# Two decoder layers on one core: early weights, identity products across barriers, a gather merged by halves, and an input scale found before the FFN

## The chip, the cores and the metric

The kernel runs on one core of a Trainium2 chip. The metric is the device time of one execution in microseconds (us); lower is better. The five engines of the core are TensorE (PE), VectorE (DVE), ScalarE (ACT), GpSimd (POOL) and SyncE (SP), which here only issues transfers.

## The reference

Sixteen sequences of 256 tokens with 256 features pass through two decoder layers. Each has self-attention (16 heads of 16 features), cross-attention to a context of 77 tokens, and a feed-forward part (FFN), each ahead of a residual sum and behind a layernorm without weights:

```python
x = x + attn(norm(x), window 64, w_qkv, w_out)     # L0 self-attention, |i - j| <= 32
x = x + xattn(norm(x), ctx, padding mask per batch) # L0 cross-attention
x = x + moe(norm(x))                                # L0 FFN: 8 experts, top 2, 256-512-512-256, gelu
x = x + attn(norm(x), causal)                       # L1 self-attention
x = x + xattn(norm(x), ctx, mask of 256 x 77)       # L1 cross-attention
x = x + ffn(norm(x))                                # L1 FFN: weights of 4 bits, activations of 16 bits
# every quantisation of the L1 FFN has one scale for the whole tensor:
scale = max(max(abs(t)) / 32767, 1e-12); q = clip(round(t / scale), -32768, 32767) * scale
```

## The kernel before

The program has five parts, each an `nc.Block` in which every engine has its own stream of instructions; at the end of a block all engines meet at a barrier. Semaphores order the engines inside a block.

1. `layers` fills constants: GpSimd clears `v_aug` and `eye` and sets the ones columns, VectorE derives `selects` and `to_all` from the identity matrix, SP loads the first item of `x`.
2. `attention(..., "window", "cross_pad", route=...)` runs layers 1 and 2 as one software pipeline and also normalises the result, finds each token's two experts and scatters its rows into regions of DRAM (`route`).
3. `experts` runs 71 tiles of 128 rows. A tile's expert weights (2.18 MB) are loaded whole into a ring of four; the first expert's parts are loaded at the end of part 2. It also quantises the raw weights of the last FFN and starts the gather of the first item's results (`gather_first`, four indirect transfers, two for each half of 128 tokens).
4. `attention(..., "causal", "cross_mask", merge=..., tail=...)` runs layers 3 and 4 in the same pipeline. It merges the experts' rows (`merge_rows`), and in its `tail` normalises the result, turns it into `x_sb` (`last_turn` on TensorE, `keep_turned` on ScalarE) and keeps a peak of absolute values for each item (`tail.peak`).
5. `quantised_ffn` finds the scale of its input from these peaks (`across`, `scale`), quantises `x`, and then runs gate, up and down products with a whole-tensor peak between each.

The attention pipeline has steps `ref` = 0, 1, ...; there are N = 32 items (16 sequences for each of two layers). In step `ref` item `ref` is projected (Q, K, V), item `ref`-1 gets its first scores and row maxima, item `ref`-2 its second scores, exponentials and P*V, item `ref`-3 its output transposes and output projection, item `ref`-4 its residual sum (`add_output`) and, in the tail, its last layernorm, and item `ref`-5 is turned. Each step has eight sub-steps `i`, and every engine runs `step(t, ref)` in this order, which is written out by hand. Sub-steps of full steps are in a hardware loop (`Fori`), the first and last ones are written out. Q and K are stacked through SP: 16 transfers a step from `parts` to `q_pair` and `k_pair`. Identity products (`keep_warm`) fill waits of TensorE at the start of part 4 (START_WARM, 16 calls), at the end of part 2 (END_WARM, 24) and in the FFN (BEFORE_GATE, 6, and others). A call is one fp32 product of 128x128 and shows as two instructions.

## Time and profile before

| | |
|---|---|
| median of 3 runs | 2162.05 us (2161.76 to 2166.89) |
| profiled execution | 2154.5 us |
| its span, first to last instruction | 2152.9 us |
| TensorE busy | 1999.5 us, 93% |
| VectorE, ScalarE, GpSimd busy | 1247.8, 964.2, 691.5 us |
| mean granted TensorE clock | 0.979 of full |
| part 1 | 0 to 5.8 us |
| part 2 | 5.8 to 659.5 us |
| part 3 | 659.5 to 1193.5 us |
| part 4 | 1193.5 to 1822.2 us |
| part 5 | 1822.2 to 2152.9 us |

The profile is of one execution. Its instructions carry start and duration, the idle time of the engine before them, and what ended that wait. A timeline merges like instructions that follow each other; "x8" is their count, and the duration then spans them all. An fp32 product shows as two instructions. TensorE's clock has two levels, 1.2 and 2.4 GHz. Queue rows (SPq) are the issue of a transfer, not its run.

### The profile page before, as it was taken

What the parts mean: (1) busy time and instruction counts of PE and PEld (TensorE: products, weight loads), DVE (VectorE), ACT (ScalarE), POOL (GpSimd) and SP (SyncE); (2) the same over time, 40 slices, a digit from 0 to 9 for tenths busy, and PEclk for the clock granted to TensorE, in tenths of its full rate; (3) what the DMA queues carried; (4) which work ended last, traced back from release to release, by engine and by line L of the source; (5) the groups of instructions that cost most, each with busy time, mean ns of one, the idle gap of its engine ahead of it and who ended that gap; (6) DMA issues with size and microseconds to landing.
All of it is one profiled execution on the core that took longest, in us unless ns stands there. A gap on an engine that the chain in (4) does not pass through costs nothing. (4 is left out here: it accounts for less than half of the span.)

```text
span 2152.9 us, 51243 instructions
## 1 busy us (share of the span) xinstructions
PE 1999.5 (93%) x17250; PEld 1544.5 (72%) x17250; DVE 1247.8 (58%) x5456; ACT 964.2 (45%) x1873; POOL 691.5 (32%) x1246
## 2 busy tenths in 40 slices
PE   7999998999968999999999889999999997999889
PEld 5777776666647999999999567777766664444377
DVE  5788886666641011111015588888778785459964
ACT  3455545666622333333333255555555553357410
POOL 3666665345561000000000555553322220013410
PEclk9999999999968999999999999999999998999999
DMA  7333333333319999999996633343223331000023
GB/s 219 107 110 103 112 110 94 93 108 116 115 60 359 370 344 341 337 350 337 341 346 242 193 123 126 124 134 112 90 89 108 105 101 36 0 0 1 0 60 97
DMA packets 209540, 334.50 MB, mean 155 GB/s; under 512 B 59501, under 2 KB 193426, under 8 KB 200306
## 3 DMA queue, kind: packets, MB, share of 16 engines
q1 hardware_dynamic: 194914, 301.82, 40.4%
q0 software_dynamic: 9552, 26.10, 4.0%
q10 hardware_dynamic: 4928, 4.72, 0.6%
q8 instruction: 82, 1.34, 0.3%
q14 instruction: 64, 0.52, 0.1%
HBM read 193.74 MB, written 28.05 MB: 103 GB/s over the span
## 5 line engine op out<-in xcount | busy, mean ns | idle before, releaser
L1978 ACT ACTIVATE moe_h<-moe_h_ps,moe_weights 128x128 f32<-128x128 f32 x424 | 132.8, 364 | 258.6 <-PE moe_h_ps L1948 226.1
L1293 ACT ACTIVATE causal_prob<-causal_ps 128x768 f32<-128x768 f32 (+1 forms) x192 | 169.0, 880 | 110.6 <-PE causal_ps L1546 109.7
L2416 PE MATMUL ffn_prod_ps<-x_sb,ffn_weights 128*128 128x512 f32 x480 | 209.2, 595 | 7.0 <-ACT ffn_sig_q L2402 7.0
L2010 DVE TENSOR_TENSOR moe_y<-moe_y_ps,moe_weights 128x256 f32<-128x256 f32 x53 | 22.5, 425 | 328.2 <-PE moe_y_ps L1960 328.2
L1891 POOL DMA_DIRECT2D moe_y_dram<-moe_y x71 | 39.4, 555 | 496.2 <-DVE moe_y L2010 496.2
L1948 PE MATMUL moe_h_ps<-moe_h,moe_weights 128*128 128x128 f32 x1696 | 198.0, 275 | 0.0
L1948 PEld LDWEIGHTS moe_h_ps<-moe_h,moe_weights 128*128 128x128 f32 x1696 | 193.6, 192 | 0.1
L2416 PEld LDWEIGHTS ffn_prod_ps<-x_sb,ffn_weights 128*128 128x128 f32 x480 | 90.5, 190 | 123.5 <-issue 109.2
L1010 DVE CUSTOM_DVE_ANT_0 causal_masked<-causal_ps,causal_causal_mask 128x256 bf16<-128x256 f32 (+1 forms) x512 | 152.4, 353 | 40.2 <-PE causal_ps L1512 38.2
L1010 DVE CUSTOM_DVE_ANT_0 window_masked<-window_ps,window_window_mask 128x160 bf16<-128x160 f32 x512 | 135.2, 319 | 58.2 <-PE window_ps L1512 55.7
L1293 ACT ACTIVATE window_prob<-window_ps 128x640 f32<-128x640 f32 x128 | 90.0, 703 | 97.1 <-PE window_ps L1546 96.2
L805 POOL TENSOR_SCALAR_AFFINE_SELECT causal_prob<-causal_prob 128x512 f32<-128x512 f32 x128 | 85.3, 691 | 115.0 <-ACT causal_prob L1293 114.9
L1512 PEld LDWEIGHTS causal_ps<-k_pair,q_pair 64*128 64x128 f32 x1024 | 72.0, 185 | 66.9 <-issue 33.1
L1512 PE MATMUL causal_ps<-k_pair,q_pair 64*128 64x78 f32 (+2 forms) x1024 | 98.1, 293 | 18.1 <-DVE causal_m_tok L1010 15.9
L2267 DVE TENSOR_REDUCE ffn_peak<-ffn_wide 128x1 f32<-128x1024 f32 x72 | 87.0, 1210 | 47.9 <-ACT ffn_wide L2376 47.9
L1512 PE MATMUL window_ps<-k_pair,q_pair 64*128 64x160 f32 (+1 forms) x1024 | 99.3, 295 | 16.2 <-DVE window_m_tok L1010 16.1
L1010 DVE CUSTOM_DVE_ANT_0 causal_masked<-causal_ps,causal_cross_mask 128x77 bf16<-128x77 f32 x512 | 86.2, 235 | 47.0 <-PE causal_ps L1512 46.9
L1512 PEld LDWEIGHTS window_ps<-k_pair,q_pair 64*128 64x128 f32 x1024 | 74.0, 187 | 49.9 <-DVE window_m_tok L1010 28.1
L1930 PE MATMUL moe_h_ps<-moe_rowsT,moe_weights 128*128 128x128 f32 x848 | 105.0, 278 | 2.5 <-DMA moe_weights<-moe_w_in 2.5
L792 POOL TENSOR_SCALAR_AFFINE_SELECT window_prob<-window_prob 128x384 f32<-128x384 f32 (+1 forms) x128 | 74.8, 608 | 94.6 <-ACT window_prob L1293 94.5
L1930 PEld LDWEIGHTS moe_h_ps<-moe_rowsT,moe_weights 128*128 128x128 f32 x848 | 100.4, 194 | 2.7 <-DMA moe_weights<-moe_w_in 2.7
L1960 PE MATMUL moe_y_ps<-moe_weights,moe_h 128*128 128x256 f32 x424 | 100.4, 380 | 0.7 <-ACT moe_h L1978 0.7
(389 smaller groups left out, 4694.2 us busy)
## 6 DMA issues: line engine op xcount, KB each, us to landing
moe_weights<-moe_w_in SPq DMA_DIRECT2D x53, 2180.0 KB, 9.3
q_pair<-parts SPq DMA_DIRECT2D x512, 128.0 KB
parts<-moe_w_in SPq DMA_DIRECT2D x17, 2180.0 KB, 9.0
k_pair<-parts SPq DMA_DIRECT2D x256, 128.0 KB
k_pair<-parts SPq DMA_DIRECT2D x256, 38.5 KB
moe_y_dram<-moe_y POOLq DMA_DIRECT2D x71, 128.0 KB, 3.5
moe_rows<-moe_slots_dram SPq DMA_DIRECT2D x53, 128.0 KB, 3.5
x_before_ffn_dram<-x_sb SPq DMA_DIRECT2D x16, 256.0 KB, 2.2
```

What stands on the lines that cost most here:

```text
L792: op = nc.gpsimd.affine_select(out=m, in_=m, compare_op=ALU.is_ge, fill=0.0, base=base, pattern=[[0, 4], [1, width]], channel_multiplier=-1)
L805: op = nc.gpsimd.affine_select(out=m, in_=m, compare_op=ALU.is_ge, fill=0.0, base=0, pattern=[[0, 4], [1, P]], channel_multiplier=-1)
L1010: op = nc.vector.tensor_tensor_reduce(masked[:, junk * width:junk * width + nk_real], ps1[:, ab, p * L.width1 + col:p * L.width1 + col + n ...
L1293: nc.scalar.activation(out, src, ACT.Exp).then_inc(expd, 1)
L1512: op = nc.tensor.matmul(ps1[:, ab, j * L.width1 + col:j * L.width1 + col + nk], q_pair[par][rows_of[ab], i + j, qt * P:qt * P + P], k_pair ...
L1891: pool.dma_start(route.y_dram[bass.ds(j * TM, TM), :].rearrange("(s p) d -> p s d", p=P), y[r][:])\
L1930: op = nc.tensor.matmul(h1_ps[:, f // 2, (f % 2) * TM:(f % 2) * TM + TM], w1[:, k, f * P:f * P + P], rowsT[:, k, :], start=(k == 0), stop= ...
L1948: op = nc.tensor.matmul(h2_ps[:, f // 2, (f % 2) * TM:(f % 2) * TM + TM], w2[:, k, f * P:f * P + P], h1[:, k, :], start=(k == 0), stop=(k ...
L1960: op = nc.tensor.matmul(y_ps[:, r % YR, s * D:s * D + D], h2[:, k, s * P:s * P + P], w3[:, k, :], start=(k == 0), stop=(k == FB - 1))
L1978: nc.scalar.activation(out[:, f, :], psum[:, f // 2, (f % 2) * TM:(f % 2) * TM + TM], ACT.Gelu, bias=bias[:, f:f + 1]).then_inc(done, 1)
L2267: return nc.vector.tensor_reduce(out, rows, AX.XY, ALU.max, apply_absolute_value=True)
L2416: op = nc.tensor.matmul(prod_ps[:, slot, f, :].rearrange("p (b t) -> p b t", b=2), w[:, k, at:at + P], x_cols(n // GROUPS, k), start=(k == ...
```

## The change

- The Q and K weights of layers 1 and 3 get tensors of their own (`first_wq`, `first_wk`). SP loads those of layer 1 in part 1, behind the first item of `x`, and those of layer 3 in part 3, at tile 7, behind the raw FFN weights. SP's other loads of part 4 stand behind the wait for the first gather's second half.
- TensorE gets identity products in part 1 (6 calls), at the head of part 2 (LOAD_WARM, 6), at the head of part 3 (FIRST_WARM, 7), and in the emptying steps of part 4 (DRAIN_WARM, 4 and 2). END_WARM goes from 24 to 13. BEFORE_GATE goes from 6 to 4 and stands at the head of part 5.
- One of the two `v_aug` tensors is filled by VectorE. In both attention parts GpSimd begins `constants()` only after the first normalisation.
- The first item's gather signals by halves of 128 tokens (`half_in`, `got_in`), and VectorE merges the first half before it waits for the second.
- In the tail's emptying steps (`emptied`, `ref` >= N + 2) the two turns of rows go to two PSUM banks (`turn_bank`), without waits between them. In step N + 3 the peak comes behind the statistics.
- The FFN's input scale is found in the last step of part 4 (`input_scale`), and kept in `tail.scales` and `tail.inverse`.
- In steps in which `ref`-1 is an item of layer 4, `add_output` comes before the first row maximum instead of after it.

```diff
 class Tail:
-    def __init__(self, rows_dram, peak):
+    def __init__(self, nc, ctx, rows_dram, peak):
         self.rows_dram, self.peak = rows_dram, peak
+        self.scales, self.inverse = (ctx.enter_context(nc.sbuf_tensor(f"ffn_{n}", [P, 5], F32)) for n in ("scales", "inverse"))
...
-        START_WARM, END_WARM = 16, 24
+        START_WARM, END_WARM, LOAD_WARM, DRAIN_WARM = 16, 13, 6, 4
...
+        def emptied(ref):
+
+            return bool(tail) and ref >= N + 2
+
+        def turn_bank(ref, k):
+
+            return ps1[:, k, 0:S] if emptied(ref) else bank(0)[:, S:2 * S]
...
+                if merge:
+                    sp.wait_ge(got_in[0], 32)
                 load_layer(0)
                 if load:
                     x_view, _, x_second, x_loaded = load
                     sp.dma_start(x_sb[:, ST:TILES // 4, :], x_view[:, ST:TILES // 4, :]).then_inc(x_second, 16)
-                if merge:
-                    sp.wait_ge(got_in[0], 64)
-                    sp.wait_ge(wq_in, 16)
...
                 layernorm(0, 0)
-                if merge:
-                    pool.wait_ge(normed, 1)
+                pool.wait_ge(normed, 1)
                 constants()
...
+                def input_scale():
+
+                    one, top_one = tail.scales[:, 0:1], row_top[:, 1:2]
+                    dve.wait_ge(peak_found, 2)
+                    nc.vector.reduce_max(whole_top[:], tail.peak[:], AX.X).then_inc(peak_found, 1)
+                    dve.wait_ge(top_turned, 1)
+                    nc.vector.reduce_max(top_one, ps2[0:1, 0, 0:P], AX.X).then_inc(top_spread, 1)
+                    dve.wait_ge(top_row, 1)
+                    nc.vector.tensor_scalar(one, ps2[:, 1, 0:1], 1.0 / QMAX, LEAST, ALU.mult, ALU.max).then_inc(top_scaled, 1)
+                    dve.wait_ge(top_scaled, 1)
+                    nc.vector.reciprocal(tail.inverse[:, 0:1], one)
...
+                    if isinstance(t, int) and t == 0:
+                        s, k = n // 2, n % 2
+                        if n % 2 == 0:
+                            dve.wait_ge((merge.half_in, got_in[0])[s], 32)
+                        else:
+                            dve.wait_ge(merged, n)
...
+                        added_first = active(ref, 4) and active(ref, 1) and layer_at(ref, 1).kind == "cross_mask"
+                        if i == 0 and added_first:
+                            add_output(t, ref, 4)
                         if active(ref, 1):
                             row_max(t, ref, i)
-                        if i == 0 and active(ref, 4):
+                        if i == 0 and active(ref, 4) and not added_first:
                             add_output(t, ref, 4)
...
-                        if i == 1 and tail and in_tail(ref, 5):
+                        if i == (3 if ref == N + 3 else 1) and tail and in_tail(ref, 5):
...
                     if ref == 0 and merge:
-                        pe.wait_ge(got_in[0], 64)
+                        pe.wait_ge(got_in[0], 32)
                         keep_warm(START_WARM)
+                    if ref == 0 and load:
+                        keep_warm(LOAD_WARM)
...
+                        if i == 3 and ref == STEPS - 1 and tail:
+                            pe.wait_ge(peak_found, 3)
+                            nc.tensor.transpose(ps2[0:1, 0, 0:P], whole_top[:], ident[:]).then_inc(top_turned, 1)
                         if i == 4 and in_tail(ref, 5):
-                            pe.wait_ge(last_ev, tail_item(t, 5) * 2 + 1)
+                            if not emptied(ref):
+                                pe.wait_ge(last_ev, tail_item(t, 5) * 2 + 1)
...
                         if i == 5 and active(ref, 3):
                             pe.wait_ge(o_ev, t - 2)
-                            if in_tail(ref, 5):
+                            if in_tail(ref, 5) and not emptied(ref):
                                 pe.wait_ge(last_ev, tail_item(t, 5) * 2 + 2)
...
                         if i == 6 and active(ref, 3):
+                            if emptied(ref):
+                                keep_warm(DRAIN_WARM, ps2)
                             pe.wait_ge(o_norm, t - 2)
...
                         if i == 7 and active(ref, 3):
+                            if emptied(ref):
+                                keep_warm(DRAIN_WARM // 2, ps2)
                             pe.wait_ge(oT_ev, t - 2)
...
+                if tail:
+                    pe.wait_ge(top_spread, 1)
+                    nc.tensor.matmul(ps2[:, 1, 0:1], ones_row[:], row_top[:, 1:2], start=True, stop=True).then_inc(top_row, 1)
...
+                        if j == RING + 3:
+                            for n, name in enumerate(("Wq", "Wk")):
+                                sp.dma_start(early[n][:], a[f"L1_attn_{name}"].rearrange("(k p) n -> p k n", p=P))\
+                                  .then_inc(early[2], 16)
...
-                                .then_inc(route.got_in, 16)
+                                .then_inc((route.half_in, route.got_in)[s], 16)
...
+                    for _ in range(FIRST_WARM):
+                        nc.tensor.matmul(h2_ps[:, 0, 0:P], ident[:], ident[:], start=True, stop=True)
                     tiles(pe, tile)
...
-BEFORE_GATE, BEFORE_PEAK, BEFORE_DOWN = 6, 20, 6
+BEFORE_GATE, BEFORE_PEAK, BEFORE_DOWN = 4, 20, 6
...
-                nc.vector.reduce_max(top[:, X_:X_ + 1], x_peak[:], AX.X).then_inc(found[0], 1)
-                across(0, 1)
-                scale(X_, 1.0)
...
+                keep_warm(BEFORE_GATE)
                 pe.wait_ge(ones_ready, 1)
-                across(0, X_, 1)
-                keep_warm(BEFORE_GATE)
...
+                for n in range(2):
+                    sp.dma_start(early[0][n][:], a["L0_attn_w_qkv"][:, n * D:n * D + D].rearrange("(k p) n -> p k n", p=P))\
+                      .then_inc(early[0][2], 16)
+
+            @block.tensor
+            def _(pe):
+                for _ in range(6):
+                    nc.tensor.matmul(first_ps[:, 0:P], ident[:], ident[:], start=True, stop=True)
...
-                for i in range(2):
-                    nc.gpsimd.memset(v_aug[i][:], 0.0)
                 nc.gpsimd.memset(eye[:], 0.0).then_inc(filled, 1)
-                pool.wait_ge(filled, 1)
-                for i in range(2):
-                    op = nc.gpsimd.memset(v_aug[i][:, :, :, HD:HD + 1], 1.0)
-                op.then_inc(filled, 1)
+                nc.gpsimd.memset(v_aug[0][:], 0.0).then_inc(filled, 1)
+                pool.wait_ge(filled, 2)
+                nc.gpsimd.memset(v_aug[0][:, :, :, HD:HD + 1], 1.0).then_inc(filled, 1)
...
+                nc.vector.memset(v_aug[1][:], 0.0).then_inc(v_zeroed, 1)
                 dve.wait_ge(filled, 1)
```

## Rows read from the trace of the kernel before

**Rows 1.** The page, part 1: the engines.

```profile
...
PE 1999.5 (93%) x17250; PEld 1544.5 (72%) x17250; DVE 1247.8 (58%) x5456; ACT 964.2 (45%) x1873; POOL 691.5 (32%) x1246
...
```

**Rows 2.** Timeline, 0 to 45 us: start, length, engine, line [idle before, releaser].

```profile
...
1.95 1.84 POOL L2533 MEMSET v_aug<- 128x1024 f32 x2 [0.31 <-POOLq L2493]
...
5.35 0.22 DVE L2553 CAST to_all<-picked 128x128 bf16<-128x128 f32 x1
...
8.17 2.70 DVE L87 TENSOR_SCALAR window_xn<-x_sb,window_mv,window_rstd 128x256 f32<-128x256 f32 x2 [1.11 <-POOL window_rstd L55]
...
12.88 3.75 PE L1668 MATMUL window_misc<-window_xT,window_window_wq 128*128 128x256 f32 x8 [0.84 <-ACT window_xT L1382]
...
19.47 2.57 SPq L609 DMA_DIRECT2D q_pair<-parts  x4
...
29.43 0.45 PE L1512 MATMUL window_ps<-k_pair,q_pair 64*128 64x160 f32 x4
...
```

**Rows 3.** Line 87 alone from 0 to 60 us: count, then ns min/median/max.

```profile
...
L87 DVE TENSOR_SCALAR window_xn<-x_sb,window_mv,window_rstd x6: 395/408/2381, 8.2 to 47.7; 128x256 f32<-128x256 f32 x6
...
```

**Rows 4.** Timeline across the barrier into the experts, 634 to 690 us.

```profile
...
650.93 8.37 PE L1445 MATMUL window_ps<-ident 128*128 128x128 f32 x48 [7.00 <-ACT moe_logits L1437]
...
661.46 0.33 SPq L1876 DMA_DIRECT2D moe_weights<-moe_w_in  x1
...
670.10 3.57 PE L1930 MATMUL moe_h_ps<-moe_rowsT,moe_weights 128*128 128x128 f32 x16 [2.47 <-DMA moe_weights<-moe_w_in]
...
679.14 1.95 PE L1930 MATMUL moe_h_ps<-moe_rowsT,moe_weights 128*128 128x128 f32 x16
...
```

**Rows 5.** Transfers of expert weights, 655 to 680 us: issue to landing.

```profile
...
DMA to landing us min/median/max: 8.6/12.8/15.9
```

**Rows 6.** One window, 680 to 1180 us: length, busy us (count), clock, DMA share.

```profile
...
680.00:1180.00 500.00, 500.00 (x3966) 482.43 (x3966) 75.42 (x161) 171.65 (x548) 37.76 (x68) 1.00 0.92 340
...
```

**Rows 7.** Timeline across the barrier into the second attention part, 1160 to 1235 us.

```profile
...
1193.58 0.95 POOL L1903 DMA_INDIRECT moe_got<-moe_y_dram,moe_got_pos  x1 [0.30 <-POOLq L1864]
...
1197.73 6.27 PE L1445 MATMUL causal_ps<-ident 128*128 128x128 f32 x32 [5.07 <-DMA moe_got<-moe_y_dram,moe_got_pos]
...
1199.85 0.95 POOL L746 DMA_INDIRECT causal_got<-moe_y_dram,causal_got_pos  x1 [0.30 <-issue]
...
```

**Rows 8.** Gathers and loads into got: issue to landing.

```profile
...
DMA to landing us min/median/max: 2.2/3.3/5.5
```

**Rows 9.** Timeline of one step of the last layer, 1746 to 1764 us, VectorE.

```profile
...
1748.96 0.24 DVE L1010 CUSTOM_DVE_ANT_0 causal_masked<-causal_ps,causal_cross_mask 128x77 bf16<-128x77 f32 x1 [1.32 <-PE causal_ps L1512]
...
1750.23 0.68 DVE L1028 TENSOR_TENSOR x_sb<-x_sb,causal_misc 128x512 f32 x1
...
```

**Rows 10.** Timeline of the same step, TensorE.

```profile
...
1751.01 1.97 PE L1668 MATMUL causal_misc<-causal_xT,causal_cross_mask_wq 128*128 128x256 f32 x8 [0.29 <-issue]
...
```

**Rows 11.** TensorE waits, 1540 to 1780 us: total us, times, longest.

```profile
...
PE causal_ps L1512 <- DVE causal_m_tok L1010: 4.4, 14, 0.5
PE causal_misc L1668 <- issue: 4.0, 13, 0.5
...
```

**Rows 12.** Timeline, 1802 to 1845 us: emptying steps, start of the FFN.

```profile
...
1804.91 1.02 ACT L1391 ACTIVATE causal_o_aug<-causal_pso 128x1024 f32<-128x1024 f32 x1 [1.77 <-PE causal_pso L1568]
...
1807.33 1.12 PE L1739 MATMUL causal_misc<-ident,causal_o_aug 64*128 64x64 f32 x16 [0.63 <-ACT x_sb L1351]
...
1811.15 3.78 PE L1763 MATMUL causal_misc<-causal_cross_mask_wo,causal_oT 128*128 128x256 f32 x8 [0.69 <-ACT causal_oT L1356]
...
1819.41 0.69 DVE L1185 TENSOR_REDUCE x_peak<-causal_last_xn 128x1 f32<-128x512 f32 x1
...
1822.35 0.17 DVE L2269 TENSOR_REDUCE ffn_top<-x_peak 128x1 f32<-128x16 f32 x1 [2.25 <-PEq L526]
...
1824.84 0.75 DVE L2274 TENSOR_SCALAR x_sb<-x_sb,ffn_inverse 128x1024 f32<-128x1024 f32 x1
...
1826.88 18.50 PE L2416 MATMUL ffn_prod_ps<-x_sb,ffn_weights 128*128 128x512 f32 x42
...
```

91 lines of the change are left out of this document (58 added, 33 removed).

## The prediction

> **What bounds the kernel now.** I read the page first. TensorE is busy for 1999.5 of 2152.9 us and no other engine reaches 60% [rows 1]. So a gain must come from TensorE's idle time, from stretches in which it runs at the lower of its two clock levels (1.2 instead of 2.4 GHz), or from the places where one part of the program ends and the next begins. I then read the timelines of these places: the start [rows 2, 3], the way into the experts and the experts [rows 4 to 6], the way into the second attention part [rows 7, 8], one step of the last layer [rows 9 to 11], and the emptying steps with the start of the FFN [rows 12]. TensorE is the engine that the others wait for in all long stages between them, so an advance at a joint should last to the end, and the terms add up.
>
> **Part A, the start.** The first block ends when VectorE has written to_all (5.35 + 0.22 = 5.57 us), after GpSimd has filled both v_aug tensors (1.84 us for two) [rows 2]. After the change GpSimd fills one and VectorE the other. Half of 1.84 us, 0.9, leaves GpSimd, and about as much is added to VectorE ahead of its own chain of 1.6 us; TensorE gets six identity products that must end before the block does. Nothing shows a VectorE memset of that size. If the two fills pass each other freely the block is 0.8 us shorter, if they exclude each other 0. I take 0.3. The reason is the normalisation: two instructions took 2.70 us [rows 2], although such an instruction has a median of 408 ns and one took 2381 [rows 3]; that was the one beside GpSimd's memsets in constants(). The change holds constants() back until this normalisation is done, so 2.38 - 0.41 = 2.0 us go. constants() itself ends about 0.4 us later than now, and what needs it (the bias product) comes far behind.
>
> For the two fills in the first block the Trainium skill has another answer: "SBUF — State Buffer", section "Who interferes with whom", says that on this chip a VectorE instruction with at most one SBUF input outside its two-port modes does not contend with GpSimd. By that rule the fills would be free of each other and part A would gain 0.5 us more than I take.
>
> TensorE thus gets its first rows 2.3 us earlier. The first eight Q products took 3.75 us at the low level; the same eight of shape 128x256 take 1.97 in [rows 10]. The identity products ahead of them (12 instructions in each of two blocks) may lift the clock: up to 1.8 us for Q and another 0.9 for K. Against this, VectorE's statistics of the second item wait for x, ahead of the low part of Q in the same queue, and SP issues the first q_pair transfer only at 19.47, right after its last load [rows 2]. Both come earlier by what leaves SP's queue in this block (two weights of about 0.5 us each) and by the shorter start: 1.8 to 2.3 us. TensorE's first scores (29.43) are then 1.8 us earlier if these loads and a low clock bind, 4.2 if nothing binds. I take **3.0**.
>
> **Part B, into the experts.** The 24 identity products take 8.37 us [rows 4] and end last before the barrier, at 659.3. Thirteen of them, all at the low level, would take about 5.8 us (26 instructions of some 0.22: the 8.37 us hold some 27 low and 21 high ones), so the barrier falls 2.5 us earlier. Seven new ones stand behind it, while the first rows are still in flight. SP's first transfer of whole expert weights starts 2.5 us earlier than 661.46, and TensorE's wait for it (2.47 us, until 670.10) ends 2.5 us earlier. In place of 2.47 us of idle there is then about 0.9, and the clock need not fall: the sixteen products took 3.57 us there and 1.95 later [rows 4], so another 1.6. Together 4.1; I take **4.0**. Lower bound 2.5 (the clock falls anyway). Upper bound 4.8: the third transfer took up to 15.9 us [rows 5], and the next layer of products at 679.14 has only some 2.7 us to spare. The two early loads of Wq and Wk (0.5 MB) go behind the raw FFN weights into the same queue. TensorE is busy for all of the 500 us from 680 on [rows 6], so I cost them at nothing; if that cover were gone they would cost some 1.3 us once.
>
> **Part C, into the second attention part.** Today TensorE waits for the four gathers until 1197.73, does 16 identity products (6.27 us) and turns the first rows right behind them [rows 7]. With the weights of layer 3 already there and SP silent until the gathers land, the last gather (issued 1193.58) has the DMA engines to itself. It took 4.1 us; such transfers take 2.2 us at the least and 3.3 in the median [rows 8], and I expect it between these. The identity products then end 0.8 to 1.9 us earlier. VectorE merges the first half meanwhile, which takes 0.9 us out of its chain, but GpSimd is busy issuing the next item's gathers until 1199.85 + 0.95 = 1200.80 and only then computes the deviation, as it does now about 0.3 us later. So the rows are normed only 0.3 us earlier, at 1202.6, and TensorE can turn them 1.2 us earlier at most. I take **0.9**, with 0 and 1.2 as bounds. The layer's other loads start later, behind the gathers; their first user comes 8 us on.
>
> **Part D, the last layer's steps.** This edit is not in the change's name: add_output moves ahead of the first row maximum where layer 4 runs, 16 steps. VectorE is idle for 1.32 us before that maximum, the addition takes 0.68 us [rows 9], and what it waits for (the output projection) is complete before the scores are. It fits into the hole. TensorE's Q products wait for the addition: 0.29 us in this step [rows 10], 4.0 us over 13 steps [rows 11]. The value is 0.29 per step, 16 x 0.29 = 4.6. Early steps show other waits, so **4.3**. The waits for the row maxima (4.4 us in 14 [rows 11]) I leave: VectorE is idle again before the maximum that starts that chain, so the chain moves with TensorE. If they went too, the part would bring 8.4; if another wait took the place, 0.
>
> **Part E, emptying steps and FFN start.** o_aug is ready at 1804.91 + 1.02 = 1805.93, but its transposes start at 1807.33, behind ScalarE's two copies of turned rows, which now have PSUM banks of their own: 1.3 us. The output projection takes 3.78 us [rows 12] where eight such products take 1.97 [rows 10]: 1.8 us, and 0.6 for the two sets of transposes before it, if the new identity products (4 and 2) hold the clock. They lie in the waits for VectorE and ScalarE. Moving the peak behind the statistics takes 0.6 us out of the chain. At the joint the peak ends at 1820.1, VectorE idles 2.25 us until 1822.35 and quantises x from 1824.84 [rows 12]. In the new order the reduction starts at once and the barrier (some 0.4 us) follows it; the chain is shorter by two small instructions and longer by a turn of rows ahead of its last product: 2.0 us saved. The first gate products wait for two identity products fewer: 0.4. Sum 6.7. What is late next is the clock: until now 12 identity instructions and the long chain lifted it about when the gate products began. Now these begin after eight. They take 18.50 / 42 = 0.44 us each [rows 12], twice that at the low level; if they run low for 1.2 to 4.6 us longer, half of it is lost, so I subtract 1.4. That gives 5.3 with the clock held, 2.8 without. I take **4.4**, nearer to the first.
>
> **The sum** is 3.0 + 4.0 + 0.9 + 4.3 + 4.4 = 16.6 us. The profiled execution took 2154.5 us (its span 2152.9 and 1.6 around it), so that one becomes 2137.9. The median of the runs shown is 7.5 us above it, 2162.05; against it I predict 2145.4.
>
> **The rivals.** *The clock stays low at the joints* (chance 0.2): A 1.8, B 2.5, C 0.5, D 4.3, E 2.8, sum 11.9, 2150.2. For it speaks that the identity products are few and that the clock fell beside 2.47 us of idle; against, that the idle stretches shrink everywhere. *Every wait goes* (0.13): A 4.2, B 4.8, C 1.2, D 8.4, E 5.3, sum 23.9, 2138.2. For it, VectorE is 0.6 us ahead in each step; against, its idle time before the second maximum eats this. *The reordering in layer 4 does nothing* (0.08): 12.3 us, 2149.8; TensorE's Q products would then wait for the turned rows instead, which are ready some 0.6 us earlier. *Slower* (0.04): the raw weights and the early loads together (2.9 MB) hold back the experts' weights. It decides once a transfer lands more than 2.7 us later than now; each tile concerned then costs 2.5 us of wait and 1.6 of low clock. Five tiles would cancel the gain, eight end at 2162 + 33 - 17 = 2178. Against it: TensorE had no idle time in 500 us [rows 6], with the raw weights in them.
>
> **Chances.** The forecast has 0.55; its own range is 2140 to 2151. The range for 8 in 10 takes in the second and third case and the bounds of the clock: 2135 to 2155. About 0.3%, 6.5 us, is what a measurement of this kernel can tell from no change. Below 2155.6 lie nearly all of the first four cases: faster 0.88, same 0.08, slower 0.04.
>
> **What the new profile would show.** A: first normalisation about 0.8 us long, first scores near 26.4. B: 26 identity instructions before the barrier, the second tile's first layer in about 1.95 us. C: the identity products behind the gathers start about 1 us earlier. D: no wait before Q in layer 4, steps of 15.55 instead of 15.85 us. E: output projection of the last item in 2 us, gate products some 5 us earlier relative to the last step. Wrong would make me: Q, K or the last projection still near 3.7 us, a new wait for weights after 670 us, or steps of layer 4 as long as before.

## The result, and the profile after

| | before | after |
|---|---|---|
| median of four runs | 2163.24 us (2161.76 to 2166.89) | 2147.17 us (2145.92 to 2150.1) |
| profiled execution, its span | 2154.5, 2152.9 us | 2145.92, 2144.3 us |
| ratio of the times | | 0.9928, 95% interval 0.9916 to 0.9940 |

By the medians the change takes 16.1 us off, and the interval of the ratio is 13 to 18 us; 16.6 were forecast, and the median lies 1.8 us above the predicted 2145.4. But the two profiled executions differ by 8.6 us only, and the sum of the prediction was made on a profile. So the first question is, stage by stage, where the time went, and the second why the pair of profiles shows half of it.

The page of the changed kernel, part 1, beside [rows 1]. TensorE is busy for nearly as long as before (2001.3 us against 1999.5), so the gain lies in its idle time.

```profile
...
PE 2001.3 (93%) x17274; PEld 1546.4 (72%) x17274; DVE 1247.5 (58%) x5456; ACT 963.5 (45%) x1873; POOL 689.7 (32%) x1244
...
```

**Part A.** Timeline of the changed kernel, 0 to 31 us, beside [rows 2, 3].

```profile
...
2.09 0.95 POOL L2605 MEMSET v_aug<- 128x1024 f32 x1
2.24 0.91 DVE L2611 MEMSET v_aug<- 128x1024 f32 x1 [2.24 <-PEq L2553]
...
7.47 0.74 DVE L87 TENSOR_SCALAR window_xn<-x_sb,window_mv,window_rstd 128x256 f32<-128x256 f32 x2 [1.11 <-POOL window_rstd L55]
...
8.45 2.39 DVE L948 TENSOR_SCALAR window_window_bq<-window_window_bq 128x2 f32<-128x2 f32 x1
...
10.90 3.78 PE L1716 MATMUL window_misc<-window_xT,first_wq 128*128 128x256 f32 x8 [1.98 <-DVE window_window_bq L948]
...
17.60 2.57 SPq L627 DMA_DIRECT2D q_pair<-parts  x4
18.46 0.88 DVE L993 SCALAR_TENSOR_TENSOR parts<-window_misc,window_window_bk,parts 128x256 fp32r<-128x256 f32 x2 [1.93 <-ACT parts L1307]
...
27.59 0.45 PE L1558 MATMUL window_ps<-k_pair,q_pair 64*128 64x160 f32 x4
...
```

In the row names, Q and K are each written to `parts` in two parts: ScalarE writes the high part, and VectorE (L993) the low part, which is what the high part leaves over. "K's low part" below is that instruction, 18.46 to 19.34 us here; it has nothing to do with the clock.

The two fills of `v_aug` ran side by side, 0.95 us on GpSimd and 0.91 on VectorE, where two on GpSimd took 1.84. By the rule of the Trainium skill ("SBUF — State Buffer", section "Who interferes with whom") they are free of each other; the trace agrees. The normalisation shrank from 2.70 to 0.74 us, as forecast. But `constants()` now begins right behind it, and VectorE's next instruction but one, the scaling of the two columns of `bq`, takes 2.39 us. It ends at 10.84 us, when the fifth of GpSimd's memsets there, which run from 8.27 us on, has ended at 10.82. Q waits 1.98 us for it. The blocking had moved on to another instruction. The first scores come 1.84 us earlier.

**Part B.** Timeline across the barrier into the experts, beside [rows 4].

```profile
...
658.01 4.99 PE L1491 MATMUL window_ps<-ident 128*128 128x128 f32 x26 [7.00 <-issue]
...
664.28 1.28 ACT L2044 ACT_TABLE_LOAD   x1 [6.18 <-PEq L544]
664.33 1.80 PE L2029 MATMUL moe_h_ps<-ident 128*128 128x128 f32 x14 [1.33 <-PEq L544]
...
674.64 2.05 PE L1994 MATMUL moe_h_ps<-moe_rowsT,moe_weights 128*128 128x128 f32 x16 [1.04 <-DMA moe_weights<-moe_w_in]
...
682.04 1.95 PE L1994 MATMUL moe_h_ps<-moe_rowsT,moe_weights 128*128 128x128 f32 x16
...
```

In the kernel before, ScalarE's first instruction behind the barrier was this one:

```profile
...
659.68 1.28 ACT L1978 ACT_TABLE_LOAD   x1 [8.65 <-PEq L526]
...
```

Thirteen products stand ahead of the barrier in place of 24, seven behind it. From the first of them to ScalarE's table load it takes 664.28 - 658.01 = 6.3 us, where it took 659.68 - 650.93 = 8.8. TensorE waits 1.04 us for weights in place of 2.47, and the second tile's first layer takes 2.05 us in place of 3.57, near the 1.95 of the third tile.

**Part C.** Timeline across the barrier into the second attention part, beside [rows 7].

```profile
...
1196.48 0.94 POOL L1967 DMA_INDIRECT moe_got<-moe_y_dram,moe_got_pos  x1 [0.30 <-POOLq L1924]
...
1199.26 6.36 PE L1491 MATMUL causal_ps<-ident 128*128 128x128 f32 x32 [3.71 <-DMA moe_got<-moe_y_dram,moe_got_pos]
...
1205.45 0.63 PE L1663 MATMUL causal_misc<-ident,causal_xn 128*128 128x128 f32 x4
...
1213.39 0.59 ACT L1349 ACTIVATE causal_cross_mask_ctxT<-causal_ps 128x512 f32<-128x512 f32 x1
...
1215.09 0.60 ACT L1349 ACTIVATE causal_cross_mask_ctxT<-causal_ps 128x512 f32<-128x512 f32 x1 [1.11 <-PE causal_ps L1504]
...
1217.13 4.80 PE L1520 MATMUL causal_ps<-causal_cross_mask_ctxT,causal_cross_mask_wk 128*128 128x462 f32 x8 [0.81 <-ACT causal_cross_mask_ctxT L1349]
...
```

From the issue of the last gather to TensorE's start it takes 1199.26 - 1196.48 = 2.8 us; it was 1197.73 - 1193.58 = 4.15. The rows are turned 16.92 us behind the last output product of the experts, where it was 18.20. But then ScalarE copies the first piece of the turned context and stands idle for 1.11 us with the second piece turned already, and the context products of layer 4, 3.11 us in the kernel before, take 4.80: the clock has fallen.

**Part D.** TensorE's waits in layer 4 of the changed kernel, 1543.48 to 1777.53 us (total us, times, longest), beside [rows 11]. These are its two largest.

```profile
...
PE causal_ps L1558 <- DVE causal_m_tok L1029: 3.9, 14, 0.5
PE causal_misc L1669 <- ACT causal_oT L1402: 1.9, 10, 0.2
...
```

The wait ahead of Q, 4.0 us in 13 times before, is not in the list any more. Each of the last ten steps takes 15.46 us; in the kernel before they take 15.82 on average.

**Part E.** Timeline of the emptying steps and the start of the FFN, beside [rows 12].

```profile
...
1803.64 0.72 PE L1791 MATMUL causal_misc<-ident,causal_o_aug 64*128 64x64 f32 x16 [0.65 <-ACT causal_o_aug L1437]
...
1806.84 1.99 PE L1819 MATMUL causal_misc<-causal_cross_mask_wo,causal_oT 128*128 128x256 f32 x8
...
1815.98 0.75 DVE L2335 TENSOR_SCALAR x_sb<-x_sb,ffn_inverse 128x1024 f32<-128x1024 f32 x1 [0.38 <-PEq L544]
...
1817.82 11.47 PE L2477 MATMUL ffn_prod_ps<-x_sb,ffn_weights 128*128 128x512 f32 x25
...
```

The transposes follow `o_aug` at once, the last output projection takes 1.99 us in place of 3.78, and the quantising of x begins 8.86 us earlier, 2.24 of which item 31's scores had brought along.

**Stage by stage.** The start of TensorE's first instruction of each stage (VectorE's for the quantising) cuts the span. Lengths in us, from the windows view of each profile. "Again" is a second profile of the same kernel (the first two experiments), "timed" a third one of the changed kernel (further down).

| up to | before | before, again | after | after, again | after, timed |
|---|---|---|---|---|---|
| first scores of part 2 | 29.43 | 28.64 | 27.59 | 26.25 | 27.54 |
| scores of item 4 | 76.63 | 76.62 | 76.62 | 83.39 | 76.62 |
| scores of item 23 | 347.33 | 347.90 | 347.12 | 347.08 | 347.22 |
| scores of item 31 | 130.23 | 138.30 | 134.22 | 134.91 | 134.53 |
| identity products at its end | 67.31 | 71.33 | 72.46 | 72.51 | 69.67 |
| first output product, part 3 | 22.53 | 22.11 | 18.51 | 18.75 | 18.45 |
| last output product | 512.17 | 512.48 | 512.01 | 512.01 | 512.02 |
| first rows turned, part 4 | 18.20 | 18.50 | 16.92 | 16.94 | 16.88 |
| first scores of part 4 | 13.95 | 13.65 | 16.41 | 16.31 | 16.43 |
| scores of item 4 | 80.46 | 81.85 | 79.74 | 80.70 | 79.72 |
| scores of item 15 | 223.34 | 223.51 | 223.30 | 223.33 | 223.32 |
| scores of item 31 | 258.19 | 258.27 | 252.63 | 252.42 | 252.85 |
| quantising of x | 45.07 | 44.55 | 38.45 | 38.35 | 38.40 |
| first gate product | 2.04 | 2.04 | 1.84 | 1.84 | 1.84 |
| end | 326.01 | 327.27 | 326.47 | 327.57 | 327.40 |

In the first pair of profiles the kernel before is (134.22 + 72.46) - (130.23 + 67.31) = 9.1 us better in layer 2 and the emptying behind it, where nothing was changed. The places that the change touches give 1.84 + 4.02 + 5.56 + 6.82 us, less 0.5 over the three stages of the way into part 4 (down to "scores of item 4").

### The profile page after: what moved, and what is told of

Read it like the earlier page. It is cut to its first block and busy times, and to the rows that moved or that the text cites. A ratio compares the mean times of both kernels' runs of the same rounds, so it can differ in the third digit from the quotient of the medians.

```text
span 2144.3 us, 51295 instructions
## 1 busy us (share of the span) xinstructions
PE 2001.3 (93%) x17274; PEld 1546.4 (72%) x17274; DVE 1247.5 (58%) x5456; ACT 963.5 (45%) x1873; POOL 689.7 (32%) x1244
```

## The experiments

**The kernel before, profiled again (before_again).** No edit.

> The kernel before, profiled a second time. In its first profile layer 2's steps are 16.28 us apart and part 3 computes its first tile's output (first moe_y) at 678.45 us less 2.9; the changed kernel's steps there are 16.65 us apart, and it loses 8.95 us between the first scores of the start and the end of part 2. Theory 1 (these two profiles met different executions of the same work): this profile of the kernel before shows steps of about 16.65 us in layer 2 as well, and a span near 2160 us, in line with its median. Theory 2 (the change itself slows layer 2): steps of 16.28 us again, a span near 2153 us.

It took 2168.73 us, its span 2167.0. The windows view from item 23's scores to item 31's (length, busy us and count of PE, PEld, DVE, ACT, POOL, then clock, DMA share, GB/s), first of the first profile, then of this one:

```profile
...
453.39:583.62 130.23, 123.63 (x1379) 89.37 (x1380) 84.48 (x330) 82.36 (x153) 76.20 (x174) 1.00 0.38 118
...
```

```profile
...
453.16:591.46 138.30, 126.75 (x1379) 91.34 (x1380) 84.49 (x330) 82.55 (x153) 76.22 (x174) 0.98 0.36 112
...
```

The same instructions and a longer stretch: the first profile had steps of 16.28 us throughout, this one 16.7 to 17.0 and two of 18.6 and 18.8 at a lower clock. Theory 1 holds, though the span was expected near 2160: the 9.1 us belong to the execution that the first profile caught and not to the change. The 27 other times measured of the kernel before say the same: none is below 2160.81 us, and the first profile's is 2154.5. Whether the changed kernel ever has such an execution is open: in its own profiles and in those of the experiments below the stretch takes 134.2 to 139.6 us. TensorE's wait for VectorE's `o_tok` is 0.4 us in the short steps and up to 1.1 in these; what sets it was not followed further.

**The changed kernel, profiled again (after_again).** No edit.

> The changed kernel, profiled a second time. Theory 1 (the steps of layer 2 vary from execution to execution): steps there anywhere from 16.28 to 16.65 us. Theory 2 (the change slows them): 16.65 us again. In part 4, ScalarE's wait of 1.11 us before its second copy of the turned context, and the context products of layer 4 at 4.80 us: if they come from where the loads of part 4 now stand, both are there again and the first scores come about 1.2 us later behind the first expert outputs than in the kernel before; if they belong to that one execution, they are gone and the first scores come about 1 us earlier.

It took 2153.98 us. Layer 2 has steps of 16.7 us again, and the way into part 4 is as in the first profile, ScalarE's stop and the low clock with it. New is the second line of the table, 83.39 us. Timelines of SP and of TensorE:

```profile
...
29.58 4.13 SPq L590 DMA_DIRECT2D x_sb<-x_in  x3
33.82 5.22 SPq L627 DMA_DIRECT2D q_pair<-parts  x4
...
```

```profile
...
26.25 0.45 PE L1558 MATMUL window_ps<-k_pair,q_pair 64*128 64x160 f32 x4 [0.84 <-DMA k_pair<-parts]
...
46.51 0.55 PE L1558 MATMUL window_ps<-k_pair,q_pair 64*128 64x160 f32 x4 [1.98 <-DMA k_pair<-parts]
...
```

SP puts the three 1 MB loads of the rest of x into its queue right behind step 0. Issuing them took 4.13 us, and the four q_pair transfers behind them 5.22, where four take 2.6 with nothing in the way. TensorE waits 1.98 us for k_pair, and the clock falls behind the wait: the steps took 20.26, 20.24 and 23.20 us instead of 18.22, 17.70 and 21.01. In this execution Q ran at the high level (1.99 us in place of 3.78), so the scores were 1.3 us earlier and met those loads.

**Part D undone (add_behind_max).**

```diff
-                        added_first = active(ref, 4) and active(ref, 1) and layer_at(ref, 1).kind == "cross_mask"
+                        added_first = False
```

> The changed kernel with part D undone: add_output stands behind the first row maximum again in layer 4. Theory (part D is worth what the wait of TensorE's Q products was, plus what follows from it): steps 18 to 30 at 15.82 us instead of 15.46, in all 4.6 to 5.6 us more from the first scores of step 16 to those of step 31. Rival (the steps became shorter for another reason, e.g. the earlier weights): steps stay at 15.46 us, 0 us.

From item 15's to item 31's scores it takes 257.51 us, 4.9 more than the mean of the changed kernel (252.63). The last ten steps are 15.79 us long, and the wait ahead of Q is back (4.1 us, 13 times). The theory holds. The 0.7 us that are left to the 258.2 of the kernel before are not of this edit.

**constants() later (constants_later).**

```diff
                 pool.wait_ge(normed, 1)
+                if route:
+                    pool.wait_ge(scaled[0], 1)
                 constants()
```

> The changed kernel with GpSimd's constants() in part 2 held back until VectorE has scaled bq too, so that neither the normalisation nor the 2.39 us scaling of bq runs beside GpSimd's memsets. Q products should start near 9.9 us instead of 10.90. Theory (SP's queue of loads, which ends at 17.5 us, sets when the first q_pair transfer is issued, 17.60): the first scores stay at 27.6 us, within 0.2. Rival (the scaling of bq sets the start): the first scores come 1.0 us earlier, or 2.5 to 3 if the clock holds through Q as well.

```profile
...
8.46 0.16 DVE L950 TENSOR_SCALAR window_window_bq<-window_window_bq 128x2 f32<-128x2 f32 x1
...
9.77 1.97 PE L1718 MATMUL window_misc<-window_xT,first_wq 128*128 128x256 f32 x8 [0.84 <-ACT window_xT L1430]
...
18.82 2.58 SPq L627 DMA_DIRECT2D q_pair<-parts  x4
...
```

The scaling of `bq` took 0.16 us, so GpSimd's memsets beside it had cost 2.2. Q starts 1.13 us earlier and at the high level, and still the first scores come at 26.65, later than the 26.25 above. Neither expectation fits: the theory had 27.6, and the rival's 1.0 us is met in number, but with Q at the high level it had 2.5 to 3. SP issued its last load at 18.43 and q_pair at 18.82. Two lines fit the six profiles up to here within 0.2 us. The first scores come 8.27 us behind the end of K's low part (29.43 = 21.16 + 8.27; 27.59 = 19.34 + 8.25) or some 7.95 us (7.8 to 8.1) behind the first q_pair issue (26.25 = 18.19 + 8.06; 26.65 = 18.82 + 7.83), whichever is later. The first binds when Q runs low, SP's queue when it runs high.

**The rest of x, one load a step (x_loads_spread).**

```diff
-                    if load and ref == 0:
-                        for n in range(1, 4):
+                    if load and ref < 3:
+                        for n in range(ref + 1, ref + 2):
```

> The changed kernel with the three 1 MB loads of the rest of x issued one behind each of steps 0, 1 and 2 of part 2 instead of all three behind step 0. In the profiles of the changed kernel the issue of the third load took up to 2.65 us and that of the next q_pair transfer up to 3.20 us, and TensorE waited 2.0 us for k_pair, at a lower clock behind it: from the first scores to those of item 4 it took 76.61, 83.39, 78.43 and 80.17 us, where the kernel before took 76.63 twice. Theory (an earlier start meets SP's queue while it is filled by these loads): no q_pair issue in step 1 above 1.2 us, no wait for k_pair, 76.6 us or a little less. Rival (the lower clock there has another cause): still 78 us or more.

It takes 82.65 us from the first scores to item 4's, as the rival says. The steps say more: the first two took 18.22 and 17.70 us, as short as any, and the third 27.05. There VectorE stood before this row of its timeline:

```profile
...
74.31 0.75 DVE L75 BATCH_NORM_STATS2 window_stats<-x_sb 128x6 f32<-128x256 f32 x2 [5.77 <-DMA x_sb<-x_in]
...
```

The edit issued the last load behind step 2, at 68.80 us, and its first user needed it before it could land. It made a wait of its own of 5.77 us, so the run decides nothing about the theory. The last two runs below put the loads behind step 1.

**Fewer identity products (fewer_identity).** FIRST_WARM 7 and DRAIN_WARM 4 become 0.

> The changed kernel without the seven identity products at the head of part 3 and without those in the emptying steps of part 4. Theory of the prediction: (1) in part 3 the clock falls, so that from the first identity product at the end of part 2 to the first output product it takes 1 to 1.6 us more than 18.5; (2) the output projection of the last item goes back from 1.99 to 3.8 us and the joint from the scores of item 31 to the quantising of x takes 40.3 to 40.9 us instead of 38.4. Rival (the products do nothing, the shorter waits alone hold the clock): 18.5 us and 38.4 us.

```profile
...
667.81 3.65 PE L1994 MATMUL moe_h_ps<-moe_rowsT,parts 128*128 128x128 f32 x16 [0.61 <-DVE moe_rowsT L2063]
...
```

```profile
...
1809.20 3.78 PE L1819 MATMUL causal_misc<-causal_cross_mask_wo,causal_oT 128*128 128x256 f32 x8 [0.69 <-ACT causal_oT L1402]
...
```

The first tile's first layer takes 3.65 us in place of 2.02, and the stage 20.18 in place of 18.57 (mean of three). The last projection is back at 3.78 us, and from item 31's scores to the quantising it takes 40.44 us, 2.0 more. Both prices of a low clock are as forecast. Each kernel with an edit has one profile; in the nine other profiles with the same products at this place the first stage takes 18.2 to 19.5 us (20.2 in freed_queues, see there).

**Identity products where they were (more_before_barrier).** END_WARM 24, LOAD_WARM 0, BEFORE_GATE 0.

> The changed kernel with END_WARM back at 24, no identity products ahead of the first block's rows in part 2 (LOAD_WARM 0), and none ahead of the gate products (BEFORE_GATE 0). Theory of the prediction: (1) from the first identity product to the first output product 2.5 us more (21.0 us); (2) Q at the start at the low level, 3.75 us, the first scores at 27.6 us as in the first profile of the changed kernel, since SP's queue bounds them; (3) the gate products begin up to 0.4 us earlier and run low for some us, which costs 0 to 1.5 us until the end of the first gate products. Rivals: (1) the barrier is set by something else, 18.5 us; (2) the clock at the start is worth 1.4 us, first scores 27.6 against 26.2; (3) the clock is up at the gate anyhow, 0.

```profile
...
661.31 7.35 PE L1491 MATMUL window_ps<-ident 128*128 128x128 f32 x48 [7.01 <-issue]
669.08 1.80 PE L2029 MATMUL moe_h_ps<-ident 128*128 128x128 f32 x14 [0.42 <-PEq L544]
...
```

(1) 24 products took 7.35 us where 13 took 4.99, but the stage grew by 1.6 us only, to 20.16, and not to the expected 21.0: behind 13 products TensorE stands 1.33 us at the barrier until another engine is there, behind 24 only 0.42. The same 24 products had taken 8.37 and 8.46 us in the two profiles of the kernel before, so this run undoes only 1.4 of the 2.45 us by which the barrier had moved; why they were shorter here was not followed. (2) The first scores come at 27.45, with Q low, as expected. That alone doesn't price the products: with them Q was low from end to end in four of the seven executions in which it started at 10.9 us, and high in all four in which it started at 9.8. (3) The gate products start 0.2 us earlier; the granted clock of their first 3 us is 0.76, in the changed kernel 0.81, in the kernel before 0.90. Against the kernel before the change thus pays 3 x (0.90 - 0.81) = 0.3 us of clock there.

**SP's loads ahead of the wait (loads_before_wait).**

```diff
+                load_layer(0)
                 if merge:
                     sp.wait_ge(got_in[0], 32)
-                load_layer(0)
```

> The changed kernel with SP's loads of layer 3 (wv, wo) issued at once in part 4, ahead of the wait for the first gather's second half, as before; all later loads stay behind the wait. From the last expert output to the turn of the first rows it takes 16.9 us, 18.2 to 18.5 in the kernel before. Theory (SP's silence lets the last gather land sooner): 0.5 to 1.2 us more, 17.4 to 18.1. Rival (the order of the merge and the 32 instead of 64 to wait for are what brought it): 16.9 still. ScalarE's stop of 0.4 to 1.1 us between copies of the turned context, and the low clock behind it: if the loads that stand close behind the gather cause it, it is smaller here; if it comes from ScalarE itself, it is there again.

```profile
...
1199.88 0.95 POOL L1967 DMA_INDIRECT moe_got<-moe_y_dram,moe_got_pos  x1 [0.30 <-POOLq L1924]
...
1204.24 5.67 PE L1491 MATMUL causal_ps<-ident 128*128 128x128 f32 x32 [5.26 <-DMA moe_got<-moe_y_dram,moe_got_pos]
...
```

The last gather is issued at 1199.88 and TensorE starts at 1204.24, 4.36 us later; with SP silent it was 2.8. The rows are turned 17.79 us behind the last output product: as the theory has it, SP's silence is worth 0.9 us there, and the rest of part C (18.35 - 17.79) 0.6. ScalarE's stop shrank to 0.1 us, and its second copy again began 18.3 us behind its table load at the head of part 4.

**The changed kernel, timed (after_timed).**

> The changed kernel, timed in five rounds beside the kernel before, as the mark for the run behind it. Summed from the stages of the profiles so far, (start 2.4 minus what steps 1 to 3 give back, way into the experts 3.7, way into part 4 0.3, layer 4 5.3, emptying and joint 6.6), it should be 13 to 18 us faster than the kernel before, near 2148 to 2150 us. If the gain of the first profile of the changed kernel was luck, it is below 10 us.

2146.31 us (2144.51 to 2149.84) against 2162.82, ratio 0.9932, interval 0.9918 to 0.9946. The gain is there again, 16.5 us.

**Other queues (freed_queues).** In part 2 ScalarE issues the context's loads and one weight before its first copy and three weights behind it, `constants()` is later, and loads 2 and 3 of the rest of x stand behind step 1. In part 4 START_WARM is 10, and

```diff
-                    gather(1, 1)
+                    gather(1, 1, range(0, 2))
                 layernorm(0, 0)
+                if merge:
+                    gather(1, 1, range(2, 4))
```

> The changed kernel with five edits. In part 2: constants() behind the scaling of bq; ScalarE issues the loads of the context and of layer 2's four weights instead of SP; the second and third load of the rest of x stand behind step 1. In part 4: GpSimd issues two of item 1's four gathers, then computes item 0's deviation, then issues the other two; START_WARM 10 instead of 16. Theory: the first scores come 8.27 us after the low part of K or 7.95 us after SP's first q_pair issue, whichever is later: with SP's queue shorter by some 5 us they come at 25.3 us when Q runs at the high clock, and steps 1 to 3 take 76.6 us; in part 4 the first rows are turned 15.0 us after the last output product instead of 16.9. Together 2.5 to 5 us faster than the changed kernel. Rival (the loads only change queues and x lands later; the shorter row of identity products leaves the clock low): start as now or later, 26.2 us or more; the turn in part 4 comes earlier but the products behind it take twice as long, 0 us in all.

2156.06 us (2151.95 to 2157.93), ratio to before 0.997 (0.9957 to 0.9982): 10 us slower than the changed kernel. The rival won, at both places.

```profile
...
5.36 0.50 ACTq L1494 DMA_DIRECT2D indow_cross_pad_ctx_rows<-ctx_in  x1
...
8.62 0.41 SPq L575 DMA_DIRECT2D x_sb<-x_in  x1
...
20.07 0.75 DVE L75 BATCH_NORM_STATS2 window_stats<-x_sb 128x6 f32<-128x256 f32 x2 [10.99 <-DMA x_sb<-x_in]
...
31.71 0.45 PE L1579 MATMUL window_ps<-k_pair,q_pair 64*128 64x160 f32 x4
...
```

```profile
...
1217.78 1.08 ACT L1360 ACTIVATE causal_cross_mask_ctxT<-causal_ps 128x512 f32<-128x512 f32 x2
1221.16 0.60 ACT L1360 ACTIVATE causal_cross_mask_ctxT<-causal_pso 128x512 f32<-128x512 f32 x1 [2.29 <-remote]
...
```

ScalarE's loads went out at 5.36 us, ahead of SP's load of x at 8.62. VectorE stood idle for 10.99 us until x was there at 19.98 (13.92 in the changed kernel), and the first scores came at 31.71. The edits in part 2 are several, but this chain shows the one that cost the time. In part 4 the turn came 14.94 us behind the last output product, 2.0 earlier, as forecast. But ScalarE then stops for 2.29 us between its copies of the context, and the first scores come 17.41 us behind the turn. The sum is 32.35 us where the changed kernel has 33.3, and with the next stage (81.35) it is 113.7 against 113.35: nothing gained. The way into the experts took 20.19 us, 1.6 more than the changed kernel. TensorE got the first whole expert weights 10.1 us behind their issue there, where it is 8.6 in the changed kernel; no edit here explains that.

**x ahead of wv and wo (x_first).** SP's load of items 1 to 3 stands behind `bk`, `constants()` is later, loads 2 and 3 of the rest of x stand behind step 1.

> The changed kernel with SP's load of items 1 to 3 of x issued ahead of wv and wo instead of behind them, constants() behind the scaling of bq, and the second and third load of the rest of x behind step 1. The rule from the runs so far: first scores at the later of (end of K's low part + 8.27) and (first q_pair issue + 7.95). x should land at about 12 us instead of 14, K's low part end at 15.0 to 16.5; the q_pair issue stays at 17.4 to 18.4, as SP has as many loads as before. So the first scores at 25.4 to 26.4 us (27.6 in the executions of the changed kernel with a low clock in Q), steps 1 to 3 in 76.6 us: 1 to 4 us faster than the changed kernel. Rival (wv and bv now land late and V waits): first scores 27 us or more, no gain.

**The same, and layer 2's weights on ScalarE's queue (x_first_two_queues).**

> The same, and ScalarE issues the four weights of layer 2 right after its copy of item 0's turned rows (about 9.6 us) instead of SP. SP's queue ends some 2.4 us earlier, so that q_pair is issued at 15 to 16.5 us and K's low part binds: first scores at 23.3 to 25 us, 1 to 2 us earlier than in the run with one queue. Rival (what the run with freed queues showed: more loads early share the DMA engines with x, or ScalarE's issues, 0.5 us each and more when the engines are full, hold up its first part of Q): first scores at 26 us or later.

2147.88 us (2143.1 to 2150.7) and 2148.48 (2147.37 to 2149.06), ratios to before 0.9923 (0.9906 to 0.9939) and 0.9925 (0.9912 to 0.9938): not to be told from the changed kernel. The first scores come at 26.02 and 26.03. That is inside the expected 25.4 to 26.4 for the first run, whose 1 to 4 us in the total did not show; for the second the rival's "26 us or later" came true. In both the stage to item 4's scores takes 76.6 us with the loads behind step 1, where with three loads behind step 0 a start at 26.2 to 26.7 us was followed by 83.39, 78.43 and 80.17 (but one at 25.33 by 76.69; the 76.6 of freed_queues follow a late start and are no test). Two of two without a loss, against one of four, speaks for the loads as the cause and doesn't prove it. The gain of the start would be 1.1 us against the mean of the changed kernel (27.13), and the spread from run to run is larger. The next wait stands in VectorE's timeline of x_first:

```profile
...
13.08 0.75 DVE L75 BATCH_NORM_STATS2 window_stats<-x_sb 128x6 f32<-128x256 f32 x2 [4.46 <-DMA window_window_bo<-L_attn_b_out_in]
...
```

x was there at 10.99 us, but these statistics wait for `bo`, the last load of layer 1, until 13.08, and K starts at 13.10. With two queues q_pair is issued 2.1 us earlier (15.18 against 17.31), and nothing follows from it. The two lines from above would give 25.3 and 25.4; they miss both by 0.6 to 0.8, and freed_queues, where they give 31.0, by 0.7. So they hold only where SP's queue is as in the changed kernel; in x_first TensorE waits 0.74 us for k_pair ahead of the scores.

## Why the prediction was right, step by step

Means of the three profiles of the changed kernel against the two of the kernel before:

| part | forecast | measured |
|---|---|---|
| A, start | 3.0 (1.8 to 4.2) | 29.04 - 27.13 = 1.9 |
| B, into the experts | 4.0 (2.5 to 4.8) | 22.32 - 18.57 = 3.75 |
| C, into part 4 | 0.9 (0 to 1.2) | 113.31 - 113.35 = 0.0, three stages |
| D, layer 4 | 4.3 (0 to 8.4) | 258.23 - 252.63 = 5.6, of it 4.9 by the edit |
| E, emptying and joint | 4.4 (2.8 to 5.3) | 46.85 - 40.24 = 6.6 |

The parts sum to 17.9 us; the steps behind the start take back 2.3 on average (0, 6.8 and 0). The two timed comparisons gave 16.1 and 16.5. So the total fits because errors cancelled: A, B and C were forecast 2.3 us too high together and D and E 3.5 too low, and the steps behind the start, which the forecast does not have, took 2.3 back. That the sum came within 0.5 us of the first comparison is luck; that the waits named in B, D and E went is not.

**A.** The lower bound came true. The first block ended 0.70 us earlier (5.84 to 5.14), where 0.3 were taken and 0.8 were the bound for fills that pass each other. SP's queue and the clock of Q set the start, as written. What failed is the step "the change holds constants() back until this normalisation is done, so 2.38 - 0.41 = 2.0 us go": they went there, and 2.2 came back at the next instruction but one, for which Q waits (constants_later). That is not the whole of the missing 1.1 us: with it undone the first scores come at 26.65, 0.5 before the mean of 27.13. The rest lies in the 3.0 itself, the middle between a start bound by SP's queue and a low clock and one bound by nothing: Q stayed low in two of the three profiles, and where it ran high SP's queue still held the first scores back to 25.3 us or later. I had not asked what stands behind the normalisation in VectorE's queue. Nor had I looked at SP's queue behind the start, where an earlier start meets the three big loads.

**B.** Right, by both of its steps. From the first identity product to the first use of the whole weights it takes 19.1 us in the kernel before and 16.7 in the changed one, 2.4 for a forecast 2.5: the barrier, and with it SP's issue, came 2.45 us earlier. From there to the first output product it takes 3.2 and 1.85 us, 1.4 for a forecast 1.6. The runs with single edits bear out both causes: 1.6 us for the products behind the barrier (fewer_identity) and 1.6 for fewer ahead of it (more_before_barrier).

**C.** The turn came 1.4 us earlier, as much as the upper bound allowed and a little more. What failed is that this advance lasts to the end. In ten of the twelve profiles of changed kernels ScalarE stops between its copies of the context and goes on 18.3 to 18.7 us behind its table load at the head of part 4, whether the piece was turned at 15.7 us (freed_queues), 17.2 (the changed kernel) or later (loads_before_wait). In the kernel before it gets there at 18.6 and 18.9 by itself. In the other two (x_loads_spread, fewer_identity) there was no stop; there the first two stages take 30.4 us against 32.15 before, but with the third 111.2 and 113.5. The third stage varies by itself: 80.5 and 81.9 us in the two profiles of the kernel before. In the ten profiles with part C as in the change the three stages take 112.7 us on average, from 111.2 to 114.2, against 112.6 and 114.0 before. So C is worth 0 to 0.6 us, and no more can be told.

**D.** The mechanism was right and the size too low. 4.9 us in 16 steps are 0.31 a step, near the row of the one step (0.29); what I took off for the early steps was no loss. The other 0.7 us are there with the edit undone too (257.5 against 258.2); of them 0.6 is TensorE's shorter wait for the row maxima, 3.8 there and 4.4 before, and why it is shorter stays open.

**E.** The working summed to 6.7 us, and 6.6 were measured. The terms are right singly too, in the first pair of profiles: 1.45 us up to the transposes (forecast 1.3), 2.4 from them to the end of the projection (1.8 and 0.6), 2.8 from there to the quantising (0.6 and 2.0), and 0.2 for the first gate product (0.4). What was mis-sized is what I took off for a low clock: 1.4 us in the gate products, which measured 0.3, and another 0.9 from 5.3 to 4.4 in case the clock was not held, which had nothing to answer to. From the first gate product to the end the changed kernel takes 0.5 us more on average (327.15 against 326.64), which is less than the 1.3 us between the two profiles of the kernel before.

Of the rivals, *the clock stays low at the joints* was seen in part A and at the copies of the context, and not at B, D and E. *Slower* did not show: from the first to the last output product of part 3 it takes 512.0 us in every profile of a changed kernel.

## What to carry to other kernels

When work is held back on one engine to free another, look up what runs beside it at its new place: the blocking moves with the work. An advance at a joint is worth what the next fixed thing leaves of it (a queue with big loads, an engine that isn't ready), so measure up to the next long stage and not up to the joint. And profile each kernel more than once before a sum is made on one execution: here steps of 16.28 or 16.7 us in untouched code hid half of the gain. Look also at where a stretch starts and ends: "the barrier came 1.4 us later" in a run with one edit undone was not what the change had moved against the kernel before (2.4).

## What the runs showed of the hardware

- VectorE's scaling of a 128x2 tile took 2.39 us beside GpSimd's memsets and 0.16 without them, while a VectorE memset of 128x1024 beside one of GpSimd took 0.91. Page and trace agree: "SBUF — State Buffer" of the Trainium skill names `tensor_scalar` among the operations that can take the shared ports.
- Four transfers that SP issues in 2.6 us took 5.22 behind three 1 MB loads.
- SP's load of items 1 to 3 landed 5.9 us behind its issue in the changed kernel and 11.4 with ScalarE's loads issued 3.3 us ahead of it.
- ScalarE stops for 0.1 to 2.3 us with its input ready and resumes at nearly one time behind the head of part 4. The cause stays open. The Trainium skill ("Runtime: NRT & Kernel Launch", section "Instruction fetch mechanics") says that each engine's code comes in blocks over a DMA queue of its own while it works. That a block came late is a guess, and the traces rather speak against it. The two queues of kind "instruction" in the DMA view have no packet from 1213.5 us until ScalarE resumes at 1215.09 (the last one began near 1211.8), though the view may not show every engine's queue. With ScalarE's instructions the same, the stop stands ahead of its second copy in the changed kernel and ahead of its third in add_behind_max. Nor is it simply SP's traffic: from 12.5 to 17.5 us behind the table load SP's transfers fill 66.8% of the DMA engines' time in the changed kernel and 47.1% in the kernel before, but 66.9% and 60.4% in the two profiles without a stop.
